# Local attention scores: the mask by eight small products, and the score session's waits ahead of the last value pass

## Chip, core and metric

One core of one Trainium2 chip runs the whole program. The metric is the device time in microseconds, the median of several runs. TensorE (PE in the rows; PEld are its weight loads), VectorE (DVE), ScalarE (ACT), GpSimd (POOL) and SyncE (SP, which issues the transfers) have queues of their own and meet at semaphores.

## What is computed

The program is a stack of adaptively normalised blocks on x of shape 16 x 256 x 128: a linear attention, six layers of local attention with a gated network behind each, a relative-position attention and an MLP. The change touches the local attention alone. Shortened, one of its six layers is:

```python
def attn_layer(x, Wqkv, qs, ksc, Wo):          # x: 16 x 256 x 128, 16 heads of 64, windows of 32
    q, k, v = split_heads(x @ Wqkv)
    q, k = rotate(l2norm(q) * qs), rotate(l2norm(k) * ksc)
    # each window of 32 queries sees its own 32 keys and the 32 before it
    sim = einsum('bhwie,bhwje->bhwij', bq, bk2) * 8.0
    mask = (it < jb) | (it > jb + 32) | (jb == -1)
    sim = where(mask, -finfo.max, sim)
    out = einsum('bhwij,bhwje->bhwie', softmax(sim), bv2)
    return out.reshape(b, n, 1024) @ Wo
```

## The kernel before

`local_layers` (line 430) runs all six layers. A layer has 16 sequences of 256 tokens; each is cut into four units, two tiles of 128 tokens times two halves of the heads (8 heads). So a layer has 64 units, and one slot of the loop starts one unit. The slots are a pipeline written out by hand: in one slot, unit u is projected, unit u-2 has its queries and keys turned and its scores made, unit u-3 has its exponentials turned and its values multiplied, u-4 is turned again and u-5 goes through the output weights. `u.has(n)` says whether the unit n slots back exists. Slots of sequences 2 to 14 run in a loop over registers, four slots a turn (`units`, line 383), the rest is written out; a layer ends in slots that project nothing.

TensorE's order in a slot (`slot`, line 601) is: keys and queries (`keys_queries`, three passes into PJ[1] and three into PJ[0], each 512 columns; lines 44 to 46 in `three_passes`); turned keys and queries of u-2 into banks TB and TA (line 572); output product of u-5 (line 640); exponentials of u-3 turned into TB (ScalarE copies them out as pT, line 832); output of u-4 turned into TA; the value projection of u into PJ[0] (`values`, line 597, again lines 44 to 46); then four waits; the mask; 64 score products (line 676); 64 value products (line 686).

The scores of eight heads of 128 queries stand in the banks SC[:, 0] and SC[:, 1], one for each parity e of the head, 4 heads x 64 keys = 256 columns each. A score product works on the array tile of 64 rows (the 64 features of a head; rows 64e to 64e+63) and 32 columns (the 32 queries of window n): eight tiles, each taking one product of each of four head pairs. The mask is put into the bank ahead of them by two products, one for each e, whose stationary operand is a selection matrix of 64 rows x 128 queries and whose moving one is the mask of 64 rows x 256 columns, both bf16 (line 669); they use array tiles of 64 rows x 128 columns.

The four waits ahead of the mask are: qk_out (queries of u-2 copied out; an earlier transpose of the slot, that of u-4, waits for the same count), and `value_waits` (line 604): pT_out (ScalarE's copy of the exponentials turned in this slot), v_ready (the values' transfers), wo_out (VectorE has added the output product). The last three are needed by the value products of line 686 alone. ScalarE copies the value projection out (line 803) when its third pass is done. VectorE takes the maxima of the scores (line 1006), ScalarE the exponentials (line 810).

Of the kernel before, what the change touches and what calls it, by code (L numbers as in the profile page):

```python
# [30 lines left out]
KEYS = 2 * WIN  # L31
# [9 lines left out]
def three_passes(nc, out, lhs, rhs, start=True, stop=True):  # L41


    nc.tensor.matmul(out, lhs[0], rhs[0], start=start, stop=False)  # L44
    nc.tensor.matmul(out, lhs[0], rhs[1], start=False, stop=False)  # L45
    return nc.tensor.matmul(out, lhs[1], rhs[0], start=False, stop=stop)  # L46
# [271 lines left out]
PR = HG // 2  # L318
UPS = 4
UPL = UPS * NB  # L320
WPT = 128 // WIN
# [108 lines left out]
def local_layers(nc, g, w):  # L430
# [3 lines left out]
    yT, ident, pick, maskb = g.yT, g.ident, g.pickb, g.maskb  # L434
    Y0 = PR * VW
    with ExitStack() as ctx:
# [4 lines left out]
        s = type("Sems", (), {n: sem(n) for n in LL_SEMS})  # L441
        v_ready = [s.v_ready0, s.v_ready1, s.v_ready2, s.v_ready3]
        lw = layer_weights(nc, ctx)
        wqkv, scb, xs, fs = lw.wqkv, lw.scb, lw.xs, lw.fs
# [4 lines left out]
        xp = [sb(f"x{n}", [128, SEQ], F32R) for n in ("high", "low")]  # L449
# [28 lines left out]
        PJ = [ps("pj0"), ps("pj1")]  # L478
        TA, TB = ps("ta"), ps("tb")
        SC, OB = ps("sc", 2), ps("ob", 2)  # L480
# [4 lines left out]
        with nc.Block() as block:  # L485
# [83 lines left out]
            def _(pe):  # L569
                def transposes(out, src):  # L570
                    for p in range(PR):
                        last = nc.tensor.transpose(out[:, p * 128:(p + 1) * 128], src(p), ident[:, :])  # L572
                    return last

                def tiles64(n, e):
                    return slice(64 * e, 64 * e + 64), slice(n * WIN, (n + 1) * WIN)

                def project(u, out, j):
                    T, hg = u.tile(0), u.half(0)
                    three_passes(nc, out[:, :], [x[:, T * 128:(T + 1) * 128] for x in xp],  # L580
                                 [x[:, j, hg * 512:(hg + 1) * 512] for x in wqkv]).then_inc(s.proj_done, 1)
# [12 lines left out]
                        pe.wait_ge(s.v_out, u.count(1, 1, 1))  # L594
                    project(u, PJ[0], 0)

                def values(u):
                    pe.wait_ge(s.rot_done, u.count(2, 0, 1))
                    project(u, PJ[0], 2)

                def slot(u):
                    rows = lambda j: lambda p: t1[:, u.par(2), j, 2 * p:2 * p + 2, :].rearrange("p a b -> p (a b)")

                    def value_waits():

                        pe.wait_ge(s.pT_out, u.count(1, 3, 1))
                        pe.wait_ge(v_ready[u.ring(3)], u.values(3))
                        if u.has(5):
                            pe.wait_ge(s.wo_out, u.count(1, 5, 1))
                        elif u.was(4):  # L610
                            pe.wait_ge(s.norm_done, u.count(1, 4, 1))
# [18 lines left out]
                    if u.has(5):  # L630
# [8 lines left out]
                        for j in range(PR):  # L639
                            last = nc.tensor.matmul(OB[:, 0, Y0:Y0 + 128], wo[:, PR * h + j, :], oT[:, u.tile(5), PR * h + j, :],  # L640
                                                    start=(j == 0), stop=(j == PR - 1), skip_group_check=True)
# [8 lines left out]
                    if u.has(4):  # L650
                        pe.wait_ge(s.norm_done, u.count(1, 4, 1))
                        if u.has(2):
                            pe.wait_ge(s.qk_out, u.count(2, 2, 2))
                        else:
                            pe.wait_ge(s.oT_out, u.count(1, 5, 1))
                            if u.has(3):
                                value_waits()
                        transposes(TA, lambda p: on[:, u.par(4), p].rearrange("q e d -> q (e d)")).then_inc(s.oT_done, 1)
                    if u.has(0):
                        values(u)  # L660
                    if u.has(2):

                        t, h2 = u.tile(2), u.half(2)
                        pe.wait_ge(s.qk_out, u.count(2, 2, 2))
                        if u.has(3):
                            value_waits()
                        for e in range(2):
                            half = slice(64 * e, 64 * e + 64)
                            nc.tensor.matmul(SC[:, e, 0:PR * KEYS], pick[half, t, :], maskb[half, :, :], start=True, stop=False,
                                             skip_group_check=True)  # L670
                        for p in range(PR):
                            for n in range(WPT):
                                for e in range(2):
                                    r, q = tiles64(n, e)
                                    k0 = t * 128 + n * WIN
                                    last = nc.tensor.matmul(SC[q, e, p * KEYS:(p + 1) * KEYS], qT[r, u.par(2), p, q],  # L676
                                                            kT[r, h2, p, k0:k0 + KEYS], start=False, stop=True,
                                                            skip_group_check=True)
                        last.then_inc(s.score_done, 1)
                    if u.has(3):  # L680

                        for p in range(PR):
                            for n in range(WPT):
                                for e in range(2):
                                    r, q = tiles64(n, e)
                                    last = nc.tensor.matmul(OB[q, e, p * VW:(p + 1) * VW], pT[r, u.par(3), p, q],  # L686
                                                            vv[r, u.ring(3), n, p, :], start=True, stop=True,
                                                            skip_group_check=True)
# [1657 lines left out]
```

## Time and profile before

| | us |
|---|---|
| median of three runs | 4032.96 (4031.32 to 4040.4) |
| profiled execution | 4037.71 |
| span in it | 4035.9 |
| busy: PE / DVE / ACT / POOL | 3736.3 / 3168.1 / 2890.0 / 2185.4 |
| mean granted TensorE clock | 0.967 |

In the views below, a row of the timeline is: start in us, length in us, engine, line, operation, output<-inputs, the array tile in rows*columns, shapes, xcount of instructions merged into it, and in brackets the idle time before it and what ended it. The lengths of matmuls are modelled and overlap; the distance between two starts is what the array took. "Issue" is idle time in which the profile shows nothing waited for.

### The profile page before, as it was taken

What the parts mean: (1) busy time and instruction counts of PE and PEld (TensorE: products, weight loads), DVE (VectorE), ACT (ScalarE), POOL (GpSimd) and SP (SyncE); (2) the same over time, 40 slices, a digit from 0 to 9 for tenths busy, and PEclk for the clock granted to TensorE, in tenths of its full rate; (3) what the DMA queues carried; (4) which work ended last, traced back from release to release, by engine and by line L of the source; (5) the groups of instructions that cost most, each with busy time, mean ns of one, the idle gap of its engine ahead of it and who ended that gap; (6) DMA issues with size and microseconds to landing.
All of it is one profiled execution on the core that took longest, in us unless ns stands there. A gap on an engine that the chain in (4) does not pass through costs nothing. (4 is left out here: it accounts for less than half of the span.)

```text
span 4035.9 us, 185445 instructions
## 1 busy us (share of the span) xinstructions
PE 3736.3 (93%) x68782; PEld 2953.1 (73%) x68782; DVE 3168.1 (78%) x9826; ACT 2890.0 (72%) x8589; POOL 2185.4 (54%) x2262
## 2 busy tenths in 40 slices
PE   6769999989999899998999999999999998699997
PEld 4437888678887688876888768888688885477773
DVE  5647888778887788877888778888788886588873
ACT  4537888568886688865888757887578884488883
POOL 3416777467774677755777557776467771300000
PEclk8879999999999999999999999999999999799998
DMA  1013333233332233332333313333233331100000
GB/s 40 6 32 79 79 79 80 65 75 79 79 79 77 61 78 80 79 84 55 78 79 79 92 49 78 79 79 79 64 77 79 79 80 26 35 0 0 0 0 27
DMA packets 305306, 246.31 MB, mean 61 GB/s; under 512 B 74485, under 2 KB 299860, under 8 KB 304340
## 3 DMA queue, kind: packets, MB, share of 16 engines
q1 hardware_dynamic: 305108, 243.72, 23.9%
q8 instruction: 118, 1.93, 0.2%
q14 instruction: 80, 0.66, 0.1%
HBM read 24.54 MB, written 2.12 MB: 7 GB/s over the span
## 5 line engine op out<-in xcount | busy, mean ns | idle before, releaser
L810 ACT ACTIVATE wa_pb<-wa_sc,wa_nm 128x64 f32<-128x64 f32 x3072 | 670.1, 329 | 403.7 <-DVE wa_nm L1006 401.5
L1156 POOL TENSOR_TENSOR wa_t<-wa_t,wa_rn 128x512 f32<-128x512 f32 x768 | 785.2, 1043 | 278.8 <-DVE wa_rn L984 278.2
L1162 POOL TENSOR_TENSOR wa_t<-wa_t 128x512 f32<-128x512 f32 x384 | 495.5, 1290 | 501.3 <-DVE wa_t L960 500.8
L958 DVE TENSOR_TENSOR wa_t<-wa_pj,wa_ctab 128x512 f32<-128x512 f32 x768 | 525.9, 685 | 257.9 <-PE wa_ta L572 219.1
L44 PE MATMUL wa_pj<-lw_wqkv_high,wa_xhigh 128*128 128x512 f32 x1152 | 536.4, 466 | 81.8 <-issue 44.8
L793 ACT ACTIVATE wa_sq<-wa_pj 128x512 f32<-128x512 f32 x768 | 488.8, 638 | 123.0 <-PE wa_pj L46 123.0
L1171 POOL TENSOR_TENSOR wa_t<-wa_t 128x512 f32<-128x512 f32 x384 | 491.0, 1279 | 0.0
L46 PE MATMUL wa_pj<-lw_wqkv_high,wa_xlow 128*128 128x512 f32 x1152 | 463.3, 402 | 0.1
L45 PE MATMUL wa_pj<-lw_wqkv_low,wa_xhigh 128*128 128x512 f32 x1152 | 460.2, 400 | 0.0
L966 DVE TENSOR_REDUCE wa_raw<-wa_sq 128x16 f32<-128x1024 f32 x384 | 449.0, 1169 | 0.0
L640 PE MATMUL wa_ob<-wa_oT,wa_wo 128*128 128x128 f32 x3072 | 409.8, 276 | 2.6 <-issue 1.6
L686 PE MATMUL wa_ob<-wa_vv,wa_pT 64*32 64x65 f32 x24576 | 367.1, 227 | 31.5 <-issue 31.5
L640 PEld LDWEIGHTS wa_ob<-wa_oT,wa_wo 128*128 128x128 f32 x3072 | 376.8, 193 | 6.2 <-issue 5.5
L676 PE MATMUL wa_sc<-wa_kT,wa_qT 64*32 64x64 f32 x24576 | 339.7, 225 | 0.0
L227 POOL TENSOR_TENSOR n_rstd<-n_mv,eps 128x4 f32<-128x4 f32 x32 | 6.4, 201 | 606.4 <-DVE n_mv L210 606.4
L44 PEld LDWEIGHTS wa_pj<-lw_wqkv_high,wa_xhigh 128*128 128x128 f32 x1152 | 218.8, 190 | 156.7 <-issue 79.8
L1006 DVE TENSOR_REDUCE wa_nm<-wa_sc 128x8 f32<-128x512 f32 x384 | 265.5, 691 | 81.2 <-PE wa_sc L676 78.6
L686 PEld LDWEIGHTS wa_ob<-wa_vv,wa_pT 64*32 64x32 f32 x24576 | 300.4, 105 | 37.8 <-issue 36.2
L959 DVE TENSOR_TENSOR wa_t<-wa_pj,wa_stab 128x256 f32<-128x256 f32 x768 | 316.5, 412 | 0.0
L960 DVE TENSOR_TENSOR wa_t<-wa_pj,wa_stab 128x256 f32<-128x256 f32 x768 | 316.3, 412 | 0.0
L676 PEld LDWEIGHTS wa_sc<-wa_kT,wa_qT 64*32 64x32 f32 x24576 | 276.7, 106 | 46.9 <-issue 0.9
L1018 DVE TENSOR_TENSOR wa_on<-wa_ob,wa_rs 128x512 f32<-128x512 f32 x384 | 261.4, 681 | 0.6
(267 smaller groups left out, 8639.9 us busy)
## 6 DMA issues: line engine op xcount, KB each, us to landing
wa_vv<-wa_vt SPq DMA_DIRECT2D x2304, 65.0 KB
wa_vv<-wa_vt SPq DMA_DIRECT2D x1152, 32.5 KB
lw_wqkv<-L_ffn_Wqkv SPq DMA_DIRECT2D x6, 1536.0 KB
lw_xs<-yT SPq DMA_DIRECT2D x96, 64.0 KB
lw_fs<-yT SPq DMA_DIRECT2D x48, 128.0 KB
lw_xs<-yT SPq DMA_DIRECT2D x96, 63.8 KB
lw_fs<-yT SPq DMA_DIRECT2D x96, 63.8 KB
wa_wo<-L_ffn_Wo SPq DMA_DIRECT2D x6, 512.0 KB, 3.9
```

Source lines behind the costliest of these rows:

```text
L44: nc.tensor.matmul(out, lhs[0], rhs[0], start=start, stop=False)
L45: nc.tensor.matmul(out, lhs[0], rhs[1], start=False, stop=False)
L46: return nc.tensor.matmul(out, lhs[1], rhs[0], start=False, stop=stop)
L640: last = nc.tensor.matmul(OB[:, 0, Y0:Y0 + 128], wo[:, PR * h + j, :], oT[:, u.tile(5), PR * h + j, :], start=(j == 0), stop=(j == PR - 1) ...
L676: last = nc.tensor.matmul(SC[q, e, p * KEYS:(p + 1) * KEYS], qT[r, u.par(2), p, q], kT[r, h2, p, k0:k0 + KEYS], start=False, stop=True, sk ...
L686: last = nc.tensor.matmul(OB[q, e, p * VW:(p + 1) * VW], pT[r, u.par(3), p, q], vv[r, u.ring(3), n, p, :], start=True, stop=True, skip_gro ...
L793: nc.scalar.activation(sq[:, j * HG:(j + 1) * HG, :], PJ[j][:, :].rearrange("p (h d) -> p h d", h=HG), ACT.Square).then_inc(s.sq_done, 1)
L810: last = nc.scalar.activation(pb[:, u.par(2), p, e, :], SC[:, e, p * KEYS:(p + 1) * KEYS], ACT.Exp, bias=nm[:, u.par(2), e, p:p + 1])
L958: nc.vector.tensor_tensor(t1[:, b, j], x, table(ctab, slice(0, HD)), ALU.mult)
L1156: nc.gpsimd.tensor_tensor(here, here, rn[:, u.par(1), j * HG:(j + 1) * HG].unsqueeze(2).broadcast_to((128, HG, HD)), ALU.mult).then_inc(s. ...
L1162: nc.gpsimd.tensor_tensor(t1[:, b, 0], t1[:, b, 0], t2[:, b, 0], ALU.add).then_inc(s.qadd_done, 1)
L1171: nc.gpsimd.tensor_tensor(t1[:, b, 1], t1[:, b, 1], t2[:, b, 1], ALU.add).then_inc(s.kadd_done, 1)
```

## The change

The value projection of a slot gets the score session's waits as an argument and does them after its second pass, ahead of its third. In slots that have both a value projection and scores, the mask is put down by eight products, one on each array tile that the scores use, with 64 x 32 of the selection matrix as stationary and the same 256 columns of the mask as moving operand. In slots without a value projection the waits stand where they stood and the mask stays in two products. The two slots' value projections that are made at a layer's end (`closing`) pass no waits.

```diff
-                def values(u):
+                def values(u, last_waits=None):
                     pe.wait_ge(s.rot_done, u.count(2, 0, 1))
-                    project(u, PJ[0], 2)
+                    T, hg = u.tile(0), u.half(0)
+                    x = [p[:, T * 128:(T + 1) * 128] for p in xp]
+                    m = [p[:, 2, hg * 512:(hg + 1) * 512] for p in wqkv]
+                    nc.tensor.matmul(PJ[0][:, :], x[0], m[0], start=True, stop=False)
+                    nc.tensor.matmul(PJ[0][:, :], x[0], m[1], start=False, stop=False)
+                    if last_waits:
+                        last_waits()
+                    nc.tensor.matmul(PJ[0][:, :], x[1], m[0], start=False, stop=True).then_inc(s.proj_done, 1)
...
-                    if u.has(0):
-                        values(u)
-                    if u.has(2):
-
-                        t, h2 = u.tile(2), u.half(2)
+                    def score_waits():
                         pe.wait_ge(s.qk_out, u.count(2, 2, 2))
                         if u.has(3):
                             value_waits()
-                        for e in range(2):
-                            half = slice(64 * e, 64 * e + 64)
-                            nc.tensor.matmul(SC[:, e, 0:PR * KEYS], pick[half, t, :], maskb[half, :, :], start=True, stop=False,
-                                             skip_group_check=True)
+
+                    if u.has(0):
+                        values(u, score_waits if u.has(2) else None)
+                    elif u.has(2):
+                        score_waits()
+                    if u.has(2):
+
+                        t, h2 = u.tile(2), u.half(2)
+                        if u.has(0):
+                            for n in range(WPT):
+                                for e in range(2):
+                                    r, q = tiles64(n, e)
+                                    nc.tensor.matmul(SC[q, e, 0:PR * KEYS], pick[r, t, q], maskb[r, :, :], start=True,
+                                                     stop=False, skip_group_check=True)
+                        else:
+                            for e in range(2):
+                                half = slice(64 * e, 64 * e + 64)
+                                nc.tensor.matmul(SC[:, e, 0:PR * KEYS], pick[half, t, :], maskb[half, :, :], start=True,
+                                                 stop=False, skip_group_check=True)
```

## Rows read from the trace of the kernel before

**Rows 1.** The page, part 1: busy us, share of the span, instructions.
```profile
PE 3736.3 (93%) x68782; PEld 2953.1 (73%) x68782; DVE 3168.1 (78%) x9826; ACT 2890.0 (72%) x8589; POOL 2185.4 (54%) x2262
```

**Rows 2.** Busy time in a stretch; columns: stretch, length, engines, clock, DMA.
```profile
860.00:3350.00 2490.00, 2388.69 (x52438) 1973.20 (x52437) 2053.95 (x5330) 1879.89 (x5515) 1669.22 (x1690) 0.99 0.30 76
```

**Rows 3.** Table of waits, whole span: us in total, times, longest.
```profile
ACT wa_pb L810 <- DVE wa_nm L1006: 401.5, 382, 1.8
...
DVE wa_t L958 <- PE wa_ta L572: 219.1, 322, 5.1
...
PEld wa_sc L669 <- issue: 144.6, 384, 0.8
```

**Rows 4.** Timeline of PE, the fourth of four slots.
```profile
1503.68 0.60 PE L572 MATMUL wa_tb<-ident,wa_pb 128*128 128x128 f32 x4
...
1504.48 0.48 PE L44 MATMUL wa_pj<-lw_wqkv_high,wa_xhigh 128*128 128x512 f32 x1
1504.79 0.39 PE L45 MATMUL wa_pj<-lw_wqkv_low,wa_xhigh 128*128 128x512 f32 x1
1505.02 0.40 PE L46 MATMUL wa_pj<-lw_wqkv_high,wa_xlow 128*128 128x512 f32 x1
1505.35 0.28 PE L669 MATMUL wa_sc<-maskb,pickb 64*128 64x256 bf16 x2
1505.57 0.80 PE L676 MATMUL wa_sc<-wa_kT,wa_qT 64*32 64x64 f32 x60
...
1506.98 0.50 PE L44 MATMUL wa_pj<-lw_wqkv_high,wa_xhigh 128*128 128x512 f32 x1
```

**Rows 5.** Timeline of PE, two narrow windows: scores up to 1505.86, scores from 1505.89.
```profile
1505.57 0.48 PE L676 MATMUL wa_sc<-wa_kT,wa_qT 64*32 64x64 f32 x33
...
1505.89 0.48 PE L676 MATMUL wa_sc<-wa_kT,wa_qT 64*32 64x64 f32 x27
```

**Rows 6.** Timeline of ACT: the copies of pT in four successive slots.
```profile
1483.95 0.60 ACT L832 ACTIVATE wa_pT<-wa_tb 128x512 f32<-128x512 f32 x1
...
1490.53 0.60 ACT L832 ACTIVATE wa_pT<-wa_tb 128x512 f32<-128x512 f32 x1
...
1497.21 0.60 ACT L832 ACTIVATE wa_pT<-wa_tb 128x512 f32<-128x512 f32 x1
...
1504.40 0.60 ACT L832 ACTIVATE wa_pT<-wa_tb 128x512 f32<-128x512 f32 x1
```

**Rows 7.** Timeline of PEld: weight loads of the value passes, fourth slot.
```profile
1504.45 0.19 PEld L44 LDWEIGHTS wa_pj<-lw_wqkv_high,wa_xhigh 128*128 128x128 f32 x1
1504.56 0.19 PEld L45 LDWEIGHTS wa_pj<-lw_wqkv_low,wa_xhigh 128*128 128x128 f32 x1
1504.80 0.19 PEld L46 LDWEIGHTS wa_pj<-lw_wqkv_high,wa_xlow 128*128 128x128 f32 x1
```

**Rows 8.** Line 609 in each slot: PE's sequencer; duration ns, first and last start.
```profile
L609 PEldq EVENT_SEMAPHORE  x1: 51/51/51, 1484.9 to 1484.9; - x1
...
L609 PEldq EVENT_SEMAPHORE  x1: 315/315/315, 1490.9 to 1490.9; - x1
...
L609 PEldq EVENT_SEMAPHORE  x1: 51/51/51, 1498.1 to 1498.1; - x1
...
L609 PEldq EVENT_SEMAPHORE  x1: 51/51/51, 1505.2 to 1505.2; - x1
```

**Rows 9.** Timeline of PE: third value passes of the other slots, one turned pb.
```profile
1484.67 0.40 PE L46 MATMUL wa_pj<-lw_wqkv_high,wa_xlow 128*128 128x512 f32 x1
...
1489.89 0.60 PE L572 MATMUL wa_tb<-ident,wa_pb 128*128 128x128 f32 x4
...
1491.24 0.40 PE L46 MATMUL wa_pj<-lw_wqkv_high,wa_xlow 128*128 128x512 f32 x1
...
1497.93 0.40 PE L46 MATMUL wa_pj<-lw_wqkv_high,wa_xlow 128*128 128x512 f32 x1
```

**Rows 10.** Groups by line and shape: busy us, mean ns, idle before and its releasers.
```profile
L669 PE MATMUL wa_sc<-maskb,pickb 64*128 64x256 bf16 x768 | 109.0, 280 | 5.9 <-ACT wa_pT L832 5.3 <-issue 0.6
```

## The prediction

> **What bounds the kernel now.** I read the busy shares first: TensorE is busy 93% of the span, VectorE 78%, ScalarE 72% [rows 1]. The local layers fill most of it; in the stretch from 860 to 3350 us the matmuls are busy 2388.7 of 2490 us at a granted clock of 0.99, that is at the upper of the two levels, 2.4 GHz [rows 2]. The table of waits then says who has slack: ScalarE waits 401.5 us for the maxima of the scores and VectorE 219.1 us for TensorE's transposes, while TensorE's own large item is 144.6 us ahead of the mask's weight loads, put down to "issue" and not to another engine [rows 3]. So TensorE's order of work sets the length of a slot, and a gap that opens or closes there moves the end, unless another engine then takes over.
>
> The timeline of one slot shows what surrounds the change [rows 4]. The three value passes start at 1504.48, 1504.79 and 1505.02, the mask's two products at 1505.35, the scores at 1505.57, the next slot's first pass at 1506.98. Two passes in a row stand 0.23 us apart; third pass to mask takes 0.33, so 0.10 us is drain and exposed weight load where the array goes from 128*128 to 64*128 tiles. Mask to scores takes another 0.22 us, although 256 columns of mask are half a pass, about 0.115 us: again some 0.10 us for going to 64*32 tiles.
>
> **The change, part by part.**
>
> *Slots concerned.* 62 of the 64 slots of a layer have both a value projection and scores; in 61 of them the values of the slot three back are multiplied too, so that all four waits move. Six layers: 366 slots. The twelve others keep the mask of before; the six with the score wait alone wait for something that an earlier transpose has already waited for, and cost nothing.
>
> *The mask as eight products.* It takes away one change of the tile shape and adds six short products with their weight loads. That eight 64*32 tiles work side by side is borne out by the scores: 33 of them, 64 columns each (0.027 us of streaming), start within 0.26 us, 8 ns apart [rows 5]; this needs three to four at once. If all eight mask tiles stream together, the mask lasts 0.115 us and one load of 32 columns, some 0.03 us: scores begin 0.14 to 0.15 us after it and not 0.22, a gain of 0.07. If only four stream at a time, it is 2 x 0.115 + 0.03 = 0.26, a loss of 0.04. I take the gain, since no pair of score products shows a conflict. The Trainium skill, "TensorE: Matmul & The Clock Gate", Part 3, gives a packed group the time of one product and about 4 ns for each further tile; by that the mask would cost 0.115 + 0.03 us and the sum would be the same as mine; four at a time would speak against the page.
>
> *The supply of instructions.* After a burst of 33 products the next 27 start 10 ns apart [rows 5], the first of them 0.06 us late: instructions that stood ready are used up, and then supply sets the pace. Six more products cost at most 6 x 0.010 = 0.06 us there. Against that, the mask's longer stay lets the supply start again before the scores have used up what stood ready, which can give back up to the 0.06 us gap and 0.05 more. The rows show neither alone. I take the mask and the supply together as a gain of 0.09 us a slot, with ends of -0.10 (a loss) and +0.13.
>
> *The waits ahead of the third pass.* This is the part that decides. The third pass needs none of the four. The late one is for pT, the transposed weights that ScalarE copies out. Its copies end at 1484.55, 1491.13, 1497.81 and 1505.00 in four successive slots [rows 6]. The third pass's weight load starts at 1504.80 in the last of them [rows 7], 0.20 us before pT is there, and the matmul at 1505.02. Now the load must stand behind the wait, with everything after it on TensorE: the mask, 64 scores and 64 value products, then the next slot's passes. VectorE's maxima, ScalarE's exponentials, and ScalarE's copy of the values (it needs the third pass) wait for that.
> How soon after pT the load can go is seen in the sequencer's own records [rows 8]. Line 609, the last wait, begins at 1484.9, 1498.1 and 1505.2 (narrower windows give 1484.87, 1498.08 and 1505.16) and lasts 0.051 us; register work for the loop's counts and the other waits (lines 606, 607) stand between. In the second slot it begins at 1490.9 (1490.86) and lasts 0.315 us, up to pT's arrival. So the gate opens about 0.37, 0.05, 0.32 and 0.22 us after pT. A load then starts some 0.025 us later and its matmul 0.11 us after that (loads at 1504.45 and 1504.56 stand 0.11 apart [rows 7]). The third matmul would truly start at 1485.05, 1491.31, 1498.27 and 1505.35 where it started at 1484.67, 1491.24, 1497.93 and 1505.02 [rows 4, 9]: later by 0.38, 0.07, 0.34 and 0.33, mean 0.28 us. Today this costs nothing, as the wait runs out beside the third pass and the drain; ScalarE's pT copy held the mask for 5.3 us in the whole run [rows 10].
> Does the stall vanish in a longer rhythm? In the second slot TensorE's transposes of the exponentials (line 572 into wa_tb) run from 1489.89 for 0.60 us [rows 9], up to 1490.49, and ScalarE copies pT from 1490.53. In the fourth they end at 1504.28 [rows 4] and the copy starts at 1504.40, held by ScalarE's own copies before it, which hang on TensorE's earlier passes. Both move with TensorE, so the stall comes back in every slot. Bounds: 0.09 us a slot if the gate always opened as fast as in the second slot (three slots 0.07, the fourth 0.16 because its pT is later), and 0.38 if always as in the first.
>
> *Sum.* 0.28 - 0.09 = 0.19 us a slot, 366 slots: 70 us. I take off 5 us for slots in which TensorE waits for another engine's late work anyhow. The profiled execution took 4037.71 us with a span of 4035.9; the runs' median is 4032.96, and to it the sum is applied: 4033 + 65 = 4098 us.
>
> **Rivals.**
>
> *Heavier.* The mask's tiles stream four at a time and supply gives nothing back: 0.28 + 0.10 = 0.38 us x 366 = 139 us, 4172 us. For it: supply sets the pace in half of the scores. Against it: the stall at the third pass leaves time in which the queue fills up.
>
> *Gate as fast everywhere.* The sequencer reaches the moved waits earlier, does its register work before pT arrives, and pT's wait is the last to open. Stall 0.09, gain 0.09: 4033 us. For it: the second slot does just that. Against it: the order in which the same waits are handled is fixed by the program, and in three slots of four pT is handled first.
>
> *Faster.* One mechanism: the array now goes from 128*128 straight to 64*32 tiles and saves the whole 0.10 us of one change of shape plus the 0.06 us pause in supply, while the gate opens fast: 0.09 - 0.16 = -0.07 us x 366 = -26 us, 4007 us. It decides from the point at which the gate opens less than about 0.10 us after pT in all slots; pT's end against the third load [rows 6, 7] leaves no room for less stall than 0.07. The Trainium skill, "TensorEngine Tiling (Array Packing)", Key Properties, says that a change of tiling mode drains TensorE; the 0.33 us against 0.23 in the rows agrees, and by that rule alone, with no wait moved, the change would be faster by 366 x 0.10 = 37 us, 3996 us.
>
> **How the numbers follow.** Forecast 0.64 (4070 to 4130 us, from gains of 0.02 to 0.13 and stalls that are right to 0.05), heavier 0.12, fast gate 0.10, faster 0.14. The range 4020 to 4150 reaches over the fast gate and into the heavier case and leaves out the faster one and the heavier end, under 2 in 10. A measurement of this kernel can tell 0.2%, 8 us. Slower by more than that: the forecast and the heavier case, 0.76. Within: most of the fast gate, 0.09. Faster: 0.15.
>
> **What would show it.** The third value pass starts 0.5 to 0.7 us after the second in three slots of four, where it was 0.23, with the gap ahead of its weight load ended by ScalarE's pT copy or by issue. The mask starts 0.33 us after it as before, the scores 0.14 to 0.15 us after the mask. From mask to the next slot's first pass it takes some 1.54 us and not 1.63. ScalarE still waits for the maxima. I am wrong if the third pass is still 0.23 us behind the second, if the scores start over 0.25 us after the mask, or if a slot is no longer although the stall is there, which would mean that TensorE was not what set its length.

## The result, and the profile after

The changed kernel took 4088.1 us (4086.45 to 4098.22, four runs) beside 4034.76 us (4031.32 to 4040.4) of the kernel before: ratio 1.014, 95% interval 1.0127 to 1.0152. It is slower by 53 us. (The 4032.96 us that the prediction starts from is the median of the first three of before's four runs.) In the profiled executions the span went from 4035.9 to 4096.4 us, 60.5 us; the profiled run of after is the slowest of its four. The mean granted clock was 0.967 and 0.968, so it does not explain the difference.

The page of after, part 1, answers to [rows 1]; the table of waits (engine, output, line <- what was waited for: us, times, longest) to [rows 3]:

```profile
PE 3750.4 (92%) x71014; PEld 2942.6 (72%) x71014; DVE 3171.3 (77%) x9826; ACT 2921.6 (71%) x8589; POOL 2185.7 (53%) x2262
```

```profile
ACT wa_pb L828 <- DVE wa_nm L1024: 389.2, 380, 1.8
DVE wa_t L976 <- PE wa_ta L572: 177.0, 244, 5.3
PEld wa_pj L606 <- issue: 154.4, 360, 0.6
...
PEld wa_sc L682 <- issue: 92.1, 372, 0.7
```

Two things are to be seen. TensorE has a new idle item, 154.4 us ahead of line 606, the third value pass, in 360 slots; and 144.6 us ahead of the mask has become 92.1 in the slots with eight products. Nothing else became the bound: ScalarE still waits about 390 us for the maxima, VectorE's waits for TensorE shrank.

The slot of after that answers to the fourth of the prediction's four (timeline of PE, then of PEld, then of ACT; columns as in [rows 4, 7, 6]):

```profile
1501.83 0.48 PE L602 MATMUL wa_pj<-lw_wqkv_high,wa_xhigh 128*128 128x512 f32 x1
1502.14 0.40 PE L603 MATMUL wa_pj<-lw_wqkv_low,wa_xhigh 128*128 128x512 f32 x1
1502.65 0.47 PE L606 MATMUL wa_pj<-lw_wqkv_high,wa_xlow 128*128 128x512 f32 x1
1503.05 0.30 PE L682 MATMUL wa_sc<-maskb,pickb 64*32 64x256 bf16 x8
1503.17 0.79 PE L694 MATMUL wa_sc<-wa_kT,wa_qT 64*32 64x64 f32 x60
...
1504.56 0.50 PE L44 MATMUL wa_pj<-lw_wqkv_high,wa_xhigh 128*128 128x512 f32 x1
```

```profile
1502.62 0.19 PEld L606 LDWEIGHTS wa_pj<-lw_wqkv_high,wa_xlow 128*128 128x128 f32 x1 [0.52 <-issue]
...
1503.05 0.11 PEld L682 LDWEIGHTS wa_sc<-maskb,pickb 64*32 64x32 bf16 x8 [0.24 <-issue]
```

```profile
1501.75 0.60 ACT L850 ACTIVATE wa_pT<-wa_tb 128x512 f32<-128x512 f32 x1
```

The second pass starts at 1502.14, the third at 1502.65: 0.51 us, where two passes stood 0.23 apart. ScalarE's copy of pT ends at 1502.35; the third load starts at 1502.62, 0.27 us after it. In the next slot it is 0.36 us, two slots further 0.34 (pT from 1508.46 and 1521.90, each 0.60 long; loads at 1509.42 and 1522.84). The matmul follows its load by 0.03 us. The mask comes 0.40 us after the third pass (0.33 before); I put these 0.07 us down to the mask's weight load, which behind a late pass is not made ahead. The scores come 0.12 us after the mask. The slot between those two is the exception:

```profile
1515.79 0.40 PE L603 MATMUL wa_pj<-lw_wqkv_low,wa_xhigh 128*128 128x512 f32 x1
1516.02 0.46 PE L606 MATMUL wa_pj<-lw_wqkv_high,wa_xlow 128*128 128x512 f32 x1
```

There the third pass is 0.23 us behind the second, with no stall, and its load at 1515.97 comes 0.06 us after pT (1515.31 + 0.60). The sequencer's records of the last moved wait (line 616) show the pattern of [rows 8], 51/51/51/311 ns:

```profile
L616 PEldq EVENT_SEMAPHORE  x4: 51/51/311, 1502.5 to 1522.8; - x4
```

**Where the time went.** I call the prediction's four slots A to D (their third passes stood at 1484.67, 1491.24, 1497.93 and 1505.02 [rows 4, 9]); they repeat with each turn of the register loop. The slot shown first above is a D, and A, B and C follow it. The distances below are medians over the loop of all six layers, worked out from the starts of the named matmuls, in us:

| | before A, B, C, D | after A, B, C, D |
|---|---|---|
| 2nd to 3rd value pass | .231 .229 .231 .231 | .508 .234 .493 .479 |
| 2nd pass to first score | .772 .771 .773 .774 | 1.026 .732 1.012 .995 |
| first score to last value product | 1.272 1.386 1.345 1.271 | 1.244 1.357 1.246 1.245 |
| 1st value pass to next slot's first pass | 2.534 2.630 3.048 2.507 | 2.766 2.564 3.191 2.702 |

The last row changes by +0.232, -0.066, +0.143 and +0.195, mean +0.126 us. From the next slot's first pass on, the rest of a slot is 4.05 us, within 0.02, in every kernel here (4.10 in B where the mask alone is changed): the stall comes back in each slot and nothing in that rest swallows it.

The local phase can be cut in three (sums over six layers, in us, from the starts of the third value passes): the first twelve slots of each layer, the rest of it (49 slots each, nearly all in TensorE's register loop), and the stretch between layers.

| | first twelve | rest, mostly loop | between layers | span |
|---|---|---|---|---|
| before | 542.1 | 1980.3 | 504.1 | 4035.9 |
| after | 557.5 | 2016.6 | 513.7 | 4096.4 |
| mask_alone (e1) | 558.1 | 1953.3 | 505.2 | 4023.6 |
| waits_alone (e2) | 548.2 | 2047.9 | 504.4 | 4110.6 |
| all_but_pT (e3) | 549.2 | 1953.3 | 507.2 | 4018.1 |
| pT_alone (e4) | 553.5 | 1968.2 | 500.6 | 4032.3 |
| mask_in_loop (e6) | 534.6 | 1953.0 | 515.7 | 4016.8 |
| before again (e7) | 531.9 | 1981.3 | 502.9 | 4022.4 |
| waits_second (e8) | 561.4 | 2084.2 | 511.6 | 4167.0 |
| 72_more (e9) | 536.2 | 1977.6 | 515.2 | 4038.8 |
| in_loop_more (e10) | 538.8 | 1953.8 | 499.6 | 3998.6 |
| change_in_loop (e11) | 540.9 | 2016.6 | 516.0 | 4086.8 |
| change_in_loop_more (e12) | 547.8 | 2016.4 | 510.5 | 4085.0 |

So the change cost 36.3 us in the middle column, 0.123 us for each of 294 slots, 15.4 us in the first twelve and 9.6 us between layers. The middle column repeats within 1 us for the same program (before, e7) and for programs with the same loop (e1, e6, e10; after, e11, e12); e3, whose loop has three waits elsewhere, takes as long as e1. The one looser case is e9, with before's loop, at 2.7 us under before. The outer columns do not repeat like this.

One slip of the texts on record: on TensorE the loop covers 56 of a layer's 62 slots that project and score (336 of 372 in six layers), six a layer are written out. "Sequences 2 to 14" is the count of SyncE and GpSimd.

### The profile page after: what moved, and what is told of

Read it like the earlier page. It is cut to its first block and busy times, and to the rows that moved or that the text cites. A ratio compares the mean times of both kernels' runs of the same rounds, so it can differ in the third digit from the quotient of the medians.

```text
span 4096.4 us, 189909 instructions
## 1 busy us (share of the span) xinstructions
PE 3750.4 (92%) x71014; PEld 2942.6 (72%) x71014; DVE 3171.3 (77%) x9826; ACT 2921.6 (71%) x8589; POOL 2185.7 (53%) x2262
## 5 line engine op out<-in xcount | busy, mean ns | idle before, releaser
L44 PE MATMUL wa_pj<-lw_wqkv_high,wa_xhigh 128*128 128x512 f32 x768 | 346.5, 451 | 68.1 <-issue 49.6
L694 PE MATMUL wa_sc<-wa_kT,wa_qT 64*32 64x64 f32 x24576 | 327.6, 223 | 0.0
L46 PE MATMUL wa_pj<-lw_wqkv_high,wa_xlow 128*128 128x512 f32 x768 | 309.2, 403 | 0.0
L45 PE MATMUL wa_pj<-lw_wqkv_low,wa_xhigh 128*128 128x512 f32 x768 | 308.4, 402 | 0.0
L694 PEld LDWEIGHTS wa_sc<-wa_kT,wa_qT 64*32 64x32 f32 x24576 | 299.7, 105 | 1.8
L821 ACT ACTIVATE wa_vt<-wa_pj 128x512 f32<-128x512 f32 x384 | 228.8, 596 | 54.9 <-PE wa_pj L606 32.5
```

## Experiments

Theory: three slots of four stall at the third pass, because the late wait for pT is followed by the handling of the others; the mask gives back 0.09 us. Rivals: the mask costs nothing or loses (tiles four at a time), or the wait for pT alone makes the stall. In some of the kernels below an instruction without work (`nop`) carries the last wait.

**The mask alone**, waits where they stood.

```diff
-                        values(u, score_waits if u.has(2) else None)
-                    elif u.has(2):
+                        values(u)
+                    if u.has(2):
                         score_waits()
+                        nc.tensor.nop(nofuse=True)
```

> The mask in eight products as in the change, but all four waits behind the third value pass where they stood before; behind them one empty instruction of TensorE's sequencer, which carries the last wait. My theory (the moved waits cost about 0.25 us a slot, the mask's tiles give back 0.09 to 0.12): faster than before by 0.12 x 366 = 44 us, ratio 0.989, the third pass again 0.23 us behind the second, scores 0.12 us behind the mask. Rival (the eight products and their supply are what costs, the waits are harmless): as slow as the change, ratio about 1.014.

Measured: 4022.24 against 4032.06 us, ratio 0.9973 (0.9961 to 0.9985). The slot in the timeline of PE:

```profile
1472.11 0.39 PE L603 MATMUL wa_pj<-lw_wqkv_low,wa_xhigh 128*128 128x512 f32 x1
1472.34 0.40 PE L606 MATMUL wa_pj<-lw_wqkv_high,wa_xlow 128*128 128x512 f32 x1
1472.67 0.30 PE L683 MATMUL wa_sc<-maskb,pickb 64*32 64x256 bf16 x8
1472.79 0.79 PE L695 MATMUL wa_sc<-wa_kT,wa_qT 64*32 64x64 f32 x60
```

Third pass 0.23 us after the second, mask 0.33 after that (going straight to 64*32 tiles costs what going to 64*128 cost), scores 0.12 after the mask. Four tiles at a time would need some 0.23 us, two times half a pass, so by this estimate all eight stream side by side. From the second pass to the first score it takes 0.677 us instead of 0.772. A loop slot is 0.092 us shorter (27.0 us over 294), as priced. But the kernel gained 10 us and not the expected 44: the first twelve slots took 16.0 us more. Something outside the slot's arithmetic is at work, and the later runs look for it.

**The waits alone**, mask in two products.

```diff
-                        if u.has(0):
+                        if False:
                             for n in range(WPT):
```

> The four waits ahead of the third value pass as in the change, the mask in two products as before. My theory: the whole stall and no gain, 0.25 to 0.28 us x 366 = 92 to 102 us slower, ratio 1.023 to 1.025. Rival (the waits are harmless, the eight products cost): ratio 1.000.

Measured: 4108.38 us, ratio 1.0185 (1.0158 to 1.0211): 76 us where 92 to 102 were expected.

```profile
1505.94 0.40 PE L603 MATMUL wa_pj<-lw_wqkv_low,wa_xhigh 128*128 128x512 f32 x1
1506.42 0.47 PE L606 MATMUL wa_pj<-lw_wqkv_high,wa_xlow 128*128 128x512 f32 x1
1506.82 0.28 PE L687 MATMUL wa_sc<-maskb,pickb 64*128 64x256 bf16 x2
1507.03 0.80 PE L694 MATMUL wa_sc<-wa_kT,wa_qT 64*32 64x64 f32 x60
```

From the second pass to the first score it takes 1.127, 0.826, 1.106 and 1.091 us in A to D, so the stall is 0.355, 0.055, 0.333 and 0.317, mean 0.265. A loop slot grew by less, 0.230 us (67.6 over 294). The missing 0.035 stands in the scores and values: from the first score to the last value product C went from 1.345 to 1.268 and B from 1.386 to 1.323, while A and D, at 1.27 from the start, stayed. It is not the pause of [rows 5] that comes back: a gap of 0.06 us after the 33rd score stands in all four slots, with and without the stall. What B and C lose is slower going later in the burst, so products that had to be supplied one by one may have had time to get ready during the stall. That is a reading; no run measured the supply by itself.

**Three waits without the one for pT ahead of the third pass**, and **the one for pT alone** there; the rest ahead of the mask. (`pT_wait` is pT's wait taken out of `value_waits`; the first two lines stand in both kernels.)

```diff
 all_but_pT
-                            value_waits()
+                            value_waits(pT=not u.has(0))
...
+                        if u.has(2) and u.has(3):
+                            pT_wait()
+                            nc.tensor.nop(nofuse=True)
 pT_alone
-                        values(u, score_waits if u.has(2) else None)
-                    elif u.has(2):
+                        values(u, pT_wait if u.has(3) else None)
+                    if u.has(2):
                         score_waits()
+                        nc.tensor.nop(nofuse=True)
```

> As the change, but of the four waits only pT's stands behind the third pass (with the empty instruction behind it); the other three and their register work are ahead of it. My theory (it is pT's late arrival that holds the third pass): no stall, as the mask alone, ratio about 0.989. Rival (the register work between second and third pass is what costs, whenever pT comes): the third pass later by 0.1 to 0.3 us, ratio 1.00 to 1.02.

> As the change, but only pT's wait stands ahead of the third pass; the other three, with their register work, are behind it with the empty instruction. My theory, with pT's gate opening 0.05 us after the copy's end: the third pass is 0.07 us late in three slots and 0.16 in the fourth, mean 0.09 x 366 = 33 us, less the mask's 44 us: ratio 0.997. If the register work behind pT is no part of the stall, it is as slow as the change, 1.014; if pT is no part of it, 0.989.

Measured, in that order: 0.9986 (0.9973 to 0.9999; 4025.02 us) and 1.0017 (1.0003 to 1.0032; 4037.77 us). With the three early waits the loop is that of the mask alone, 1953.3 us: their register work costs nothing at that place. Both fell short of the 0.989 and 0.997 expected, as the mask alone did. With pT's alone, the third load waits for ScalarE in every slot and starts 0.05 us after its copy (median), but it holds up the pass in one slot of four:

```profile
1480.18 0.40 PE L603 MATMUL wa_pj<-lw_wqkv_low,wa_xhigh 128*128 128x512 f32 x1
1480.44 0.50 PE L606 MATMUL wa_pj<-lw_wqkv_high,wa_xlow 128*128 128x512 f32 x1
1480.87 0.30 PE L687 MATMUL wa_sc<-maskb,pickb 64*32 64x256 bf16 x8
```

but only by 0.03 us (0.262 from pass to pass in D, 0.234 in the others). The loop is 14.9 us longer than with the mask alone, 0.051 us a slot, and most of that is behind the third pass, where the mask's load is exposed: 0.43 us to the mask in D and 0.36 to 0.37 in the others, not 0.33. So neither the early waits (0.00) nor pT's (0.05) makes the 0.215 us that all four cost (2016.6 - 1953.3 over 294). The stall needs both: pT's wait first, and the others' counts and waits to be handled behind it before the load may go. With all four, the load starts 0.24 to 0.36 us after pT in three slots; with pT's alone, 0.05.

**The waits ahead of the second pass.**

```diff
-                    nc.tensor.matmul(PJ[0][:, :], x[0], m[1], start=False, stop=False)
                     if last_waits:
                         last_waits()
+                    nc.tensor.matmul(PJ[0][:, :], x[0], m[1], start=False, stop=False)
```

> As the change, but the four waits stand ahead of the second value pass instead of the third. My theory: the wait opens at a time that pT sets, so what stands behind it adds to the stall: one more pass, 0.23 us a slot, 366 slots, 84 us more than the change, ratio 1.035 against before; in the third of the four slots of the loop, where the third pass was only 0.06 us late, the second pass is now late by 0.29. Rival (the stall is a fixed cost of handling the waits, wherever they stand): as the change, 1.014.

Measured: 4161.02 us, 1.0329 (1.031 to 1.0347).

```profile
1531.22 0.47 PE L602 MATMUL wa_pj<-lw_wqkv_high,wa_xhigh 128*128 128x512 f32 x1
1532.02 0.47 PE L605 MATMUL wa_pj<-lw_wqkv_low,wa_xhigh 128*128 128x512 f32 x1 [0.32 <-ACT wa_pT L850]
1532.32 0.40 PE L606 MATMUL wa_pj<-lw_wqkv_high,wa_xlow 128*128 128x512 f32 x1
```

The second pass now starts 0.80 us after the first, and the idle time before it, 0.32 us, is put down to pT's copy. One pass earlier (0.23 us) costs 67.6 us in the loop, 0.230 us a slot. The stall was worked out from pT's arrival, which does not move with the waits, and the run says so one for one. It also repeats the 0.07 us behind a late pass one place earlier: the third pass now stands 0.31 us behind the second, not 0.23, and the mask is back at 0.33 behind the third.

**Where the outer columns come from.** Inside the value products of the written-out slots TensorE stops for long gaps, and its instructions between two of them can be counted. The timeline of PE in the third layer, before, and then after:

```profile
1365.35 0.41 PE L686 MATMUL wa_ob<-wa_vv,wa_pT 64*32 64x65 f32 x18 [1.24 <-issue]
...
1387.94 0.33 PE L686 MATMUL wa_ob<-wa_vv,wa_pT 64*32 64x65 f32 x12 [2.00 <-issue]
...
1411.46 0.31 PE L686 MATMUL wa_ob<-wa_vv,wa_pT 64*32 64x65 f32 x7 [1.52 <-issue]
```

```profile
1403.54 0.24 PE L704 MATMUL wa_ob<-wa_vv,wa_pT 64*32 64x65 f32 x1 [1.72 <-issue]
...
1427.59 0.34 PE L704 MATMUL wa_ob<-wa_vv,wa_pT 64*32 64x65 f32 x15 [2.24 <-issue]
```

Busy time between the three gaps of before (stretch, length, PE, PEld, DVE, ACT, POOL, clock, DMA share, GB/s):

```profile
1365.34:1387.93 22.59, 20.59 (x495) 17.50 (x496) 17.74 (x45) 17.82 (x56) 17.37 (x19) 1.00 0.33 81
1387.93:1411.45 23.52, 21.86 (x494) 18.69 (x494) 17.72 (x45) 16.64 (x51) 15.66 (x16) 0.93 0.29 69
```

495 matmuls and 496 loads, with the sequencer's own instructions between them, are 1024; so are the next stretch's. Counted over all 13 traces (loads, matmuls and sequencer's instructions, from start to start), there are 212 distances between neighbouring gaps of over 0.5 us inside scores and values in the first twelve slots of the layers. Every one is a multiple of 256: 74 times 256, 52 times 768, 84 times 1024 and twice 2048. The page's DMA queues (queue: packets, MB, share) have one for instructions:

```profile
q8 instruction: 118, 1.93, 0.2%
```

```profile
q8 instruction: 123, 2.02, 0.2%
```

Before stands first. 118 packets in 1.93 MB are 16 KB each, 64 bytes for each of 256 instructions; a packet took 0.9 to 1.6 us. Of the 23 gaps in the first twelve slots of before, the 18 longest (1.37 to 2.31 us from start to start) each begin with such a packet still running, whose end comes 1.1 to 1.6 us before TensorE goes on. And where no packets come there are no gaps: of the 118, one falls into the middle column's 294 slots, where a turn of the loop has 1352 instructions, 650 matmuls and 649 loads among them (the loop's first turn, in which gaps still fall, belongs to the first twelve slots).

Not every block end costs. In the first twelve slots of before's third layer, TensorE passes most block ends inside scores or values in 0.01 to 0.06 us and stops at four, for 1.46, 2.21, 1.73 and 0.82. Nor is a slower stretch safe: in the third layer of after one stop stands between two projection passes.

```profile
1378.51 0.46 PE L44 MATMUL wa_pj<-lw_wqkv_high,wa_xhigh 128*128 128x512 f32 x1 [1.99 <-issue]
```

The Trainium skill, "Runtime: NRT & Kernel Launch", section Instruction fetch mechanics, says that instructions come in blocks of 256, that TensorE holds 2048 of them, and that crossing a block's end is mostly hidden. The distances agree with the first, and the loop's 1352 instructions without a gap fit the second, which no run tests. In a written-out burst of small products the gaps of 1.24, 2.00 and 1.52 us do not agree with the third.

The outer columns hold two things besides the slots' own cost: these stops, and time that TensorE spends at the lower of the two clock levels (1.2 GHz). Sums in us, worked out from the traces; stops from start to start, in the first twelve slots all that stand at a block end, between the layers those inside scores and values:

| | first twelve: stops | at 1.2 GHz | between layers: stops | at 1.2 GHz |
|---|---|---|---|---|
| before | 40.4 | 46.9 | 0 | 28.2 |
| after | 55.8 | 31.9 | 9.7 | 36.4 |
| mask_alone (e1) | 58.8 | 53.2 | 5.4 | 21.9 |
| waits_alone (e2) | 35.1 | 35.2 | 0 | 19.4 |
| all_but_pT (e3) | 58.1 | 39.2 | 7.9 | 25.6 |
| pT_alone (e4) | 59.5 | 38.2 | 0 | 23.3 |
| mask_in_loop (e6) | 37.0 | 36.8 | 10.5 | 38.3 |
| before again (e7) | 39.8 | 19.9 | 0 | 24.5 |
| waits_second (e8) | 44.4 | 29.5 | 8.4 | 35.4 |
| 72_more (e9) | 39.3 | 23.9 | 11.9 | 23.9 |
| in_loop_more (e10) | 39.8 | 34.1 | 2.4 | 10.2 |
| change_in_loop (e11) | 37.4 | 27.3 | 11.1 | 30.7 |
| change_in_loop_more (e12) | 38.8 | 43.7 | 9.0 | 31.4 |

The stops go with the program: before and e7, the same program, have them alike. They account for the 9.6 us of the change between the layers (9.7 in five stops that before does not have) and are 15.4 us more in its first twelve slots; there the slots' own 0.123 x 72 = 9 us come on top, and 15 us less at the lower clock, some 5 us by the estimate below, go off. That makes some 20 us where 15.4 were measured. The 16.0 us that the mask alone lost there are 18.4 us more of stops, less what its slots gained.

The clock goes with the execution. In before and e7 the first twelve slots of the first layer are the same instructions (windows as above, the clock third from the end):

```profile
303.61:395.24 91.63, 83.91 (x1874) 69.94 (x1872) 69.53 (x176) 66.78 (x201) 62.56 (x63) 0.94 0.32 79
```

```profile
301.37:389.24 87.87, 79.98 (x1874) 66.60 (x1872) 70.41 (x177) 66.90 (x201) 62.67 (x63) 1.00 0.33 83
```

Before stands first: 3.8 us longer at a granted clock of 0.94. Beside the experiments before ran 75 times; without one run of 6966 us these go from 4020 us at a mean clock of 0.974 to 4041 at 0.969 (the lowest clock is 0.966, at 4040), and a straight line through them (correlation 0.90) gives 0.31 us for each us at the lower level.

Every instruction that the change adds (six products and six loads a slot) shifts all later block ends. Five runs were made to test that.

**The mask in the loop alone** (written-out slots as before), and **nothing but 12 empty instructions** in the written-out slots of the kernel before.

```diff
 mask_in_loop, against mask_alone
-                        nc.tensor.nop(nofuse=True)
-                        if u.has(0):
+                        if u.has(0) and u.loop is not None:
+                            nc.tensor.nop(nofuse=True)
+                        if u.has(0) and u.loop is not None:
 12_empty, against before
+                        if u.has(2) and u.loop is None:
+                            for _ in range(12):
+                                nc.tensor.nop(nofuse=True)
```

> The mask in eight products only in the slots of the register loop (52 of a layer's 62), in two products in the written-out slots; all waits behind the third pass as before, the empty instruction only in the loop. My theory now: the mask alone gains 0.10 us in each slot of the loop (312 slots, 31 us), and the first run fell short of its 44 us because the written-out slots at a layer's start grew by 2.65 us a layer: their longer instruction stream meets the borders of its 256-instruction blocks at worse places. Then this kernel is faster than before by 31 us, ratio 0.992, with the layer starts as long as before. Rival (the shortfall of the first run lies in the loop or elsewhere): ratio 0.997 as there.

> The kernel before, with twelve empty sequencer instructions added behind the key and query passes of each written-out slot: as many more instructions as the eight-product mask adds, and none that works. My theory (the place of the 256-instruction borders in the stream costs, not the mask's products): the layer starts grow by some 2.6 us as with the mask, 16 us over six layers, ratio 1.004, and TensorE's long gaps fall at the same instruction numbers as in the change. Rival (the mask's products themselves cost there): ratio 1.000.

Measured: 0.9985 (0.9973 to 0.9996; 4021.29 against 4027.41 us), and 1.0002 (0.9991 to 1.0014; 4028.5 us). The second tells nothing of block ends: the empty instructions are not in the program that ran (185445 instructions in the trace, as before). It serves as the kernel before run under another name, and shows that its first twelve slots take 542.1 us in one profiled execution and 531.9 in another, with 27 us less at the lower clock. The first moved its loss: the first twelve slots are 7.5 us shorter than before, and the stretch between layers 11.6 us longer, with 10.5 us of stops there, so it too fell short of the 0.992 expected.

**72 instructions more a layer that wait for nothing**: 12 waits on a condition long met in each written-out slot, with the kernel before, and with the mask in the loop alone.

```diff
+                        if u.has(2) and u.loop is None:
+                            for _ in range(12):
+                                pe.wait_ge(s.pads, 1)
+                                nc.tensor.nop(nofuse=True)
```

> The kernel before with twelve sequencer waits on a condition long met, behind the key and query passes of each of a layer's six written-out slots (the twelve empty instructions of the earlier run turned out not to be in the program at all, so that it measured the kernel before against itself). They add 72 instructions a layer and no work. My theory (long gaps at the borders of 256-instruction blocks are instruction transfers, and what counts is where in a slot a border falls): TensorE's gaps of over 1 us move to other slots, and the first twelve slots of a layer change by 1 us or more in either direction while the loop after its first turn stays at 329.9 us; total within 15 us of before. Rival (the gaps belong to what the slots do, not to the stream): they stay in the same slots with the same lengths, total 0 to 4 us more.

> The mask in eight products in the register loop only, as in the earlier run, with the same 72 added sequencer waits a layer in the written-out slots. My theory: the loop after its first turn keeps its 4.3 us a layer under before; the rest differs from the earlier run only by where the block borders fall. If the 12 us that the layers' ends gave back there are due to that, they change here. Range by the theory 0.990 to 1.001. Rival: 0.9985 again, all stretches as there.

Measured: 1.0031 (1.0021 to 1.0041; 4044.33 against 4032.98 us), and 0.9935 (0.9912 to 0.9958; 4000.47 us). The same instructions make the kernel before 11 us slower, and they take the kernel with the mask in the loop from 6 to 33 us under the kernel before measured beside it. The loop's time is not what moves (1977.6 and 1953.8 us). Work that costs by its amount could not do both; a shift of block ends can, and the stops are seen to move: with before 11.9 us of them appear between the layers, with the mask in the loop they fall there from 10.5 to 2.4. In the profiled spans of the second pair it is 18.2 us (4016.8 and 3998.6), of which 16.1 stand between the layers: 8.1 of stops, and 28 us less at the lower clock, some 9 us at 0.31. This is the fastest kernel of the study; one of its seven runs took 4031.43 us, at a granted clock of 0.92.

**The whole change in the loop alone**, without and with those 72.

```diff
-                        values(u, score_waits if u.has(2) else None)
-                    elif u.has(2):
+                        values(u, score_waits if u.has(2) and u.loop is not None else None)
+                    if u.has(2) and not (u.has(0) and u.loop is not None):
                         score_waits()
...
-                        if u.has(0):
+                        if u.has(0) and u.loop is not None:
```

> Both parts of the change, but only in the 56 slots a layer of TensorE's register loop; the six written-out slots as before. My theory by now: of the change's 57 us, 36 to 41 come from the loop (0.12 us a slot: 0.23 for the waits, less 0.10 for the mask) and the rest from where the borders of the instruction blocks fall. Then the loop after the first twelve slots of a layer takes 2017 us in all six layers as with the change, and the total is before + 41 us with -10 to +12 for the borders: ratio 1.007 to 1.013. Rival (the written-out slots pay for the waits and the products themselves): they drop out fully and the total is 1.009 whatever the borders do.

> The same with the 72 added sequencer waits a layer in the written-out slots, which shift the borders. My theory: the loop part again 2017 us; the layers' ends, which took 11.6 us less with these 72 waits than without when only the mask was in the loop, do so again if the gap was there without them: 4 to 12 us under the kernel without the 72, ratio 1.004 to 1.010. Rival: no difference between the two kernels.

Measured: 1.0136 (1.0121 to 1.0152; 4091.41 against 4037.02 us) and 1.0091 (1.0077 to 1.0105; 4072.06 us). Both have the loop of after, 2016.6 and 2016.4 us. With the written-out slots left as they were the kernel is as slow as with the whole change, just above the 1.013 expected: their own cost is gone, but the stops between the layers are there. With the 72 it is 35 us slower than before. Slots that carry the change are 336 here, 41 us at 0.123 each, or 1.0%. Of the 19 us between the two medians the clock has a part: e12's two runs at 0.967 and 0.968 took 4086.76 and 4083.11 us, its three at 0.971 to 0.973 some 4072, and all four of e11, 4088.82 to 4096.23, ran at 0.967 to 0.969. At a like clock, by the estimate above, the two kernels differ by some 8 us. So the slots' own cost, 0.123 us in each of 366, is 45 us or 1.1% with the whole change, and the rest of the 1.4% depends on where the written-out code's block ends lie.

## Why the prediction came out as it did

**What bounds.** Right. What TensorE lost or won between a slot's first value pass and the next slot's first pass is found again in the loop's length within 0.01 us a slot (0.126 and 0.123 for the change, 0.230 and 0.230 for the waits alone), and no other engine took over.

**The stall.** The mechanism and the pattern held, and it comes back in each slot. The size held by luck. Predicted was a third pass late by 0.38, 0.07, 0.34, 0.33 for A to D, mean 0.28, with the mask 0.33 us behind it as before. The waits alone put the first score later by 0.355, 0.055, 0.333, 0.317, mean 0.265, but the third pass itself only by 0.28, 0.00, 0.26, 0.25, mean 0.20. The load goes when it was said to: 0.36, 0.07, 0.35 and 0.24 us after pT (medians over the loop), where gate and 0.025 us make 0.395, 0.075, 0.345 and 0.245. But from load to matmul it takes 0.03 us (0.05 in B) and not 0.11; the 0.11 was the distance of two loads, and the first value pass stood 0.03 us behind its load in the rows already (1504.45 and 1504.48 [rows 7, 4]). Against that stands the 0.05 to 0.07 us more between third pass and mask, which the prediction put at nothing. Two errors of 0.07 to 0.08 us cancel. The handling of the waits behind pT's is the greater part of the stall: pT's alone costs 0.05, and of the bound of 0.09 us for that case only 0.01 us is lateness of the pass; the rest is again behind the pass.

**The mask.** Right: scores 0.12 us after the mask, where 0.14 to 0.15 was said and 0.213 stood before; all eight tiles at once. The 0.09 us a slot, of which 0.07 were the mask and 0.02 the supply, measured 0.092, but the parts are others: 0.095 from the second pass to the first score, and nothing on average in the scores and values behind it (A and D gain 0.02, C loses 0.04). From the mask to the next slot's first pass it takes 1.51 us in the D shown, where 1.54 was said. The rival of four at a time falls. The rule on changes of tiling mode (the Trainium skill, "TensorEngine Tiling (Array Packing)", Key Properties) was weighed for 0.10 us a slot with no wait moved, 37 us and 3996 us. The mask alone shows 0.092 us, which agrees, and the kernel took 4022, as the stops grew.

**The net of a slot.** Here a term was mis-sized. The forecast was 0.28 - 0.09 = 0.19 us; the loop shows 0.123. Measured terms: a stall of 0.265, of which 0.035 comes back in the scores and values, and with the mask together another 0.01 to 0.02. The prediction counted what the supply gives back on the mask's side only and never asked what a stall gives back in the products behind it. In B, where there is no stall, the whole is a gain of 0.066.

**The sum.** 0.19 x 366 gave 70 us, 65 after the 5 taken off for slots that wait anyhow (no run here shows them); with 0.123 it would have been 45. The medians differ by 53 and the profiled executions by 60.5 us. The missing 8 to 16 us are in the first twelve slots and between the layers, and this the prediction had nowhere: the instructions added shift the block ends, for 25 us more of stops in the profiled execution, of which less time at the lower clock takes a part back. So the total was right in part by luck: an overrated net and an unseen cost balance.

**The rivals.** "Heavier" needed tiles four at a time: shown false. "Gate as fast everywhere" is what runs when pT's wait stands alone there: then the kernel is 1.0017, no difference worth the name, as the 4033 us of that rival said (the slots save 0.041 us each, and 19 us more of stops in the first twelve take that back); with all four waits it is not what happens. "Faster" asked for a gate under 0.10 us after pT in all slots: in three the load starts 0.24 us and more after it.

**What stays open.** Why TensorE passes most block ends without a stop and stops at others for 0.5 to 2.7 us, what makes the granted clock differ between executions of one program, and whether stops bring on time at the lower clock, no run here settles. That the mask's exposed load is what makes the 0.07 us behind a late pass was not tested by itself. All four waits ahead of the third pass with pT's as the last was not tried; the runs suggest, without showing it, that it would cost some 0.05 us a slot as pT's alone.

## To carry over

A wait moved ahead of work that does not need it costs the lateness of the one that comes last plus the time to handle all waits queued behind it, and exposes the next weight load: look at the sequencer's own records, not at the waits' number. Putting the late one last should help, but was not tried. Where products are tiny, compare kernels over the uniform part of a loop, as the written-out part gains or loses tens of microseconds by where its blocks of 256 instructions end, and compare the granted clocks too; a median of the whole cannot price an edit of under half a percent there. The mask on the tiles that the scores use is worth having with the waits left in place: 0.9973 in all slots, and 0.9935 (0.9912 to 0.9958) in the loop alone with the block ends shifted.

## What the runs showed of the hardware

- TensorE stops for 0.5 to 2.7 us inside bursts of small products of written-out code, although no branch is near. All 212 distances counted in 13 traces are multiples of 256 instructions; the transfers are 16 KB each on the queue for instructions, 118 before and 123 after. 72 more instructions a layer are worth +11 us in one kernel and some -26 us in another.
- Eight mask tiles of 64*32 with 256 columns take 0.12 us to the next product, about half of the 0.23 us of a pass with 512 columns.
- A loop of 1352 instructions a turn shows no such gaps from its second turn on.
- A wait ahead of a weight load lets it go 0.05 us after the awaited copy when it stands alone, and 0.24 to 0.36 us after it when three more waits with their counts stand behind it.
- Executions of one kernel from 4020 to 4041 us go with mean granted clocks from 0.974 down to 0.966.
